# Attention scores with the mask on the moving keys, in a one-core windowed attention and top-1 expert kernel

## What is computed

```python
q = (x @ wq.T + bq).reshape(B, S, H, D)      # k, v likewise
loc = einsum('bnihd,bnjhd->bnihj', qw, kw) * scale          # 32 windows of 128
gsc = einsum('bihd,bjhd->bihj', q[:, gi], k[:, gi]) * scale # gi: 64 global tokens
attn = softmax(scores)          # zeros outside windows and globals
out = einsum('bihj,bjhd->bihd', attn, v) @ wo.T + bo
x = layernorm(x + out)
# experts: argmax of x @ Wg.T picks one of 8; layernorm, scale, bias,
# 256 -> 64, gelu, 64 -> 256; added to x, layernorm again
```

## Time and profile before

| what | value |
|---|---|
| median of 3 executions | 445.81 us (444.01 to 446.04) |
| span of the profiled execution, first to last instruction | 442.8 us |
| the profiled execution's own time | not listed beside its span |
| mean granted clock of TensorE | 0.989 |
| attention steps 2 to 31 | about 46 to 299 us |
| experts | about 299 to 443 us |

### The profile page before, as it was taken

How to read it: one execution, slowest core, us unless ns; L and a number is a source line. 1 busy time by engine, 2 the same in 40 slices (tenths; PEclk the granted TensorE clock), 3 DMA queues, 4 the chain that set the end, 5 groups by cost and what they waited for, 6 DMA issues and landing times.

```text
span 442.8 us, 14658 instructions
## 1 busy us (share of the span) xinstructions
PE 405.3 (92%) x5747; PEld 339.8 (77%) x5747; DVE 326.1 (74%) x796; ACT 250.6 (57%) x523; POOL 220.4 (50%) x301
## 2 busy tenths in 40 slices
PE   5899799999999999999999899988798998999991
PEld 4758678888888888888888778756577887777891
DVE  6785687758757757757759888563668998899785
ACT  3424665675575575575576576676663555544421
POOL 4361343464464464464464566435733485477540
PEclk9999999999999999999999999999989999999997
DMA  8663740000000000000020000000000011011004
GB/s 240 186 199 111 240 137 4 27 25 0 24 24 0 24 24 0 24 24 0 24 72 4 25 2 3 3 1 2 0 2 2 1 49 47 0 47 49 34 15 143
DMA packets 21720, 20.34 MB, mean 46 GB/s; under 512 B 3133, under 2 KB 21682, under 8 KB 21682
## 3 DMA queue, kind: packets, MB, share of 16 engines
q1 hardware_dynamic: 16900, 15.07, 10.9%
q10 hardware_dynamic: 4782, 4.75, 3.3%
HBM read 15.41 MB, written 4.41 MB: 45 GB/s over the span
## 4 chain that ended last, share of the span: by engine, by line
PE 52%; DVE 26%; ACT 9%; issue 8%; DMA 3%; ACTq 1%; DVEq 0%; POOL 0%; POOLq 0%
DVE row_max_t L1154 10%; PE ps L1461 7%; PE ps L1737 7%; PE ps L1424 7%; PE ps L1562 5%; PE ps L1384 5%; PE ps L1415 4%; PE ps L1438 3%; PE ps L1444 3%; ACT probs L847 3%; DVE k_part L1013 2%; ACT boundsT_t L858 2%; PE ps L1406 2%; DMA rows<-in_L_attn_x_dram 2%; ACT k_part L713 2%
## 5 line engine op out<-in xcount | busy, mean ns | idle before, releaser
L847 ACT ACTIVATE probs<-ps 128x1024 f32<-128x1024 f32 x64 | 62.1, 1022 | 68.2 <-PE ps L1428 68.2
L1154 DVE TENSOR_REDUCE row_max_t<-ps 128x16 f32<-128x2048 f32 x31 | 70.9, 2287 | 3.7 <-PE ps L1415 3.6
L1737 PE MATMUL ps<-w_part,hm_part 128*128 128x256 f32 x384 | 53.8, 289 | 1.8 <-DVE hm_part L1332 1.8
L1415 PE MATMUL ps<-k_part,q_part 32*128 32x128 f32 x1584 | 51.5, 274 | 3.1 <-issue 1.5
L1415 PEld LDWEIGHTS ps<-k_part,q_part 32*128 32x128 f32 x1584 | 46.9, 186 | 9.2 <-issue 7.0
L1562 PE MATMUL ps<-xh_parts,w_part 128*128 128x512 f32 x192 | 53.8, 416 | 0.0
L557 POOL TENSOR_TENSOR q_part<-qf,q_part 128x512 fp32r<-128x512 f32 x32 | 41.0, 1281 | 25.7 <-ACT q_part L695 25.7
L599 POOL TENSOR_TENSOR attn_t<-num_t,rden_t 128x256 f32<-128x256 f32 x32 | 20.0, 624 | 64.7 <-DVE rden_t L1185 64.7
L1737 PEld LDWEIGHTS ps<-w_part,hm_part 128*128 128x128 f32 x384 | 48.2, 190 | 4.8 <-DVE hm_part L1332 2.4
L788 ACT ACTIVATE ffn_rows<-ps,b1s 128x512 f32<-128x512 f32 x32 | 22.0, 687 | 42.2 <-PE ps L1562 34.1
L1562 PEld LDWEIGHTS ps<-xh_parts,w_part 128*128 128x128 f32 x192 | 34.7, 194 | 6.5 <-issue 0.6
(11 more groups left out here) (234 smaller groups left out, 906.4 us busy)
## 6 DMA issues: line engine op xcount, KB each, us to landing
table<-rest_sums SPq DMA_DIRECT2D x4, 1088.0 KB, 6.1
xs<-in_L_attn_x_dram SPq DMA_DIRECT2D x16, 256.0 KB, 2.8
rows<-in_L_attn_x_dram ACTq DMA_DIRECT2D x4, 1024.0 KB, 8.1
out_dram<-yout SPq DMA_DIRECT2D x6, 512.0 KB, 2.9
w<-in_L_ffn_W_dram SPq DMA_DIRECT2D x2, 256.0 KB, 7.6
w<-in_L_ffn_W_dram SPq DMA_DIRECT2D x1, 512.0 KB, 4.2
out_dram<-yout SPq DMA_DIRECT2D x2, 256.0 KB, 2.6
out_dram<-yout ACTq DMA_DIRECT2D x2, 256.0 KB, 2.8
```

What stands on the lines that cost most here:

```text
L847: act.activation(probs[:, 2 * h:2 * h + 2, :], ps[:, 2 * h:2 * h + 2, :], ACT.Exp).then_inc(probs_ready, 1)
L1154: dve.tensor_reduce(row_max[:], ps_all, op=ALU.max, axis=AX.X).then_inc(max_ready, 1)
L1415: last = mm(ps[:, u, (2 * c + a) * P:(2 * c + a + 1) * P], q_part[x][quad(u), s, c, a, :], k_part[y][quad(u), s, c, :], start=(i == 0), st ...
L1737: mm(y, hm_part[a][:, 1 - p, f, c * P:(c + 1) * P], w2_part[b][:, f, :], start=(f == 0 and i == 0), stop=False)
```

## The change

Scores: queries are kept whole (`q_whole`, not masked) as the stationary side, and the keys move in two masked copies (`k_masked`, 256 columns): 24 products. The global tokens keep the old form (`scores_of_globals`, 48). Turned scores are as before.

Masks move from DVE to POOL: eight multiplications by a column of `q_scale` per pair of windows (512 elements a partition each), two for each of the high and low part, for keys and queries. `q_low` and the copy of `qf` go. ACT writes the high part of the whole queries from PSUM (two instructions, in the even step, ahead of the exponentials); DVE writes the low part (two instructions, behind the guards).

Order in odd steps: the keys' low part on DVE comes behind the guards; on PE the output product comes ahead of turned scores, and values behind them, next to the second values. On POOL in odd steps the wait for the step's scores and the keys' high part comes first, and the argument of the exponent comes behind a wait for the keys' low part.

`k_masked` lies in a part of `xh_parts`, so the first casts of the expert input move from step 30 to step 31. `w1` lies in `ysum`, so its two loads move from the start to step 24, ahead of `w2`, and its scaling and splitting one step later.

```diff
+        k_masked = [xh_parts[:, 0, i].rearrange("p c n -> p (c n)").rearrange("p (w c a n) -> p w c a n", w=2, c=KC, a=2)
+                    for i in range(2)]
...
-        qf = sb("qf", [P, 2, KC, 2, P])
+        q_whole = [sb(f"q_whole{i}", [P, SLOTS, KC, P], fp32r) for i in range(2)]
...
@@ SP, step 24 (and no longer at the start)
                     sp.wait_ge(rest_ready, NW // 2 + 1)
+                    for c in range(KC):
+                        sp.dma_start(w1[:, c, :, :], w1_dram[:, c * P:(c + 1) * P, :].rearrange("e p h -> p e h")).then_inc(ld_w1, 16)
...
@@ POOL
-            def q_low(w, s):
-                need(pool, turned_scores_in_psum, w - 3)
-                pool.wait_ge(q_high_ready, w // 2 + 1)
-                pool.tensor_tensor(q_part[1][:, s], qf[:, s % 2], q_part[0][:, s].bitcast(fp32), ALU.subtract).then_inc(q_ready, 1)
+            def await_keys_high(w):
+
+                need(pool, scores_in_psum, w)
+                pool.wait_ge(k_high_ready, w // 2 + 1)
...
+            def mask_keys(i, s):
+                for a in range(2):
+                    pool.tensor_scalar(k_masked[i][:, :, :, a, :], k_part[i][:, s:s + 2].bitcast(fp32), q_scale[:, a, 0:1], None,
+                                       ALU.mult).then_inc(k_masked_ready, 1)
+
+            def mask_queries(i, s):
+                for a in range(2):
+                    pool.tensor_scalar(q_part[i][:, s:s + 2, :, a, :], q_whole[i][:, s:s + 2].bitcast(fp32), q_scale[:, a, 0:1], None,
+                                       ALU.mult).then_inc(q_masked_ready, 1)
...
+                keys_due = live(t + 1, steady) and p
+                queries_due = cur and p == 0 and (steady or t > 0)
+                if keys_due:
+                    await_keys_high(t + 1)
+                if queries_due:
+                    await_queries(t)
                 if pp:
...
-                if live(t + 1, steady) and (steady or t > 0):
-                    q_low(t + 1, (s + 1) % SLOTS)
+                if keys_due:
+                    mask_keys(0, (s + 1) % SLOTS)
+                if queries_due:
+                    mask_queries(0, s)
                 if cur:
...
+                    if keys_due:
+                        await_keys_low(t + 1)
                     need(pool, e_ready, t - 1)
...
+                if keys_due:
+                    mask_keys(1, (s + 1) % SLOTS)
+                if queries_due:
+                    mask_queries(1, s)
...
-            q_low(0, 0)
-            q_low(1, 1)
+            pool.wait_ge(dve_const, 4)
+            await_keys_high(0)
+            mask_keys(0, 0)
+            await_keys_low(0)
+            mask_keys(1, 0)
+            await_queries(0)
+            for i in range(2):
+                mask_queries(i, 0)
...
@@ ACT
-                need(act, turned_scores_in_psum, w - 2)
-                act.wait_ge(qf_ready, w // 2 + 1)
-                copy(q_part[0][:, s:s + 2], qf[:]).then_inc(q_high_ready, 1)
+                need(act, turned_scores_in_psum, w - 3)
+                act.wait_ge(q_in_psum, w // 2 + 1)
+                for c in range(KC):
+                    last = act.activation(q_whole[0][:, s:s + 2, c, :], ps_xq[:, c * 2 * P:(c + 1) * 2 * P].rearrange("p (w n) -> p w n", w=2),
+                                          ACT.Identity, bias=bq_col[:, c:c + 1])
...
-                if live(t + 1, steady) and p:
-                    queries_of(t + 1, (s + 1) % SLOTS)
...
+                if ahead and p == 0:
+                    queries_of(t + AHEAD, (s + AHEAD) % SLOTS)
                 if prev:
                     need(act, pv_in_psum, t - 1)
...
@@ DVE
+            def queries_of(w, s):
+
+                dve.wait_ge(q_high_ready, w // 2 + 1)
+                for c in range(KC):
+                    last = dve.scalar_tensor_tensor(q_whole[1][:, s:s + 2, c, :], ps_xq[:, c * 2 * P:(c + 1) * 2 * P].rearrange("p (w n) -> p w n", w=2),
+                                                    bq_col[:, c:c + 1], q_whole[0][:, s:s + 2, c, :].bitcast(fp32), ALU.add, ALU.subtract)
...
-                if live(t + 1, steady) and p:
-                    keys_of(t + 1, (s + 1) % SLOTS)
...
-                    queries_of(t + AHEAD)
+                    queries_of(t + AHEAD, (s + AHEAD) % SLOTS)
+                if live(t + 1, steady) and p:
+                    keys_of(t + 1, (s + 1) % SLOTS)
...
-                if not steady and t == NW - 2:
+                if not steady and t == NW - 1:
                     for pair in range(2):
                         take_high(0, 0, pair)
-                if not steady and t == NW - 1:
                     for k in range(ROUTE_STEPS):
                         route(k, 0)
...
+                    dve.wait_ge(ld_w1, 16 * KC)
...
@@ PE
             def scores(s):
 
                 for c in range(KC):
+                    for i, (x, y) in enumerate(SPLIT):
+                        for u in range(UNITS):
+                            last = mm(ps[:, u, 2 * c * P:(2 * c + 2) * P], q_whole[x][quad(u), s, c, :],
+                                      k_masked[y][quad(u), s % 2, c, :, :].rearrange("p a n -> p (a n)"),
+                                      start=(i == 0), stop=(i == 2), tile_position=(32 * u, 0))
+                return last
...
-                    pe.wait_ge(q_ready, t + 1)
-                    pe.wait_ge(k_ready, t // 2 + 1)
+                    pe.wait_ge(q_ready, t // 2 + 1)
+                    pe.wait_ge(k_masked_ready, 4 * (t // 2 + 1))
...
-                if live(t + 1, steady) and p:
-                    values_of(t + 1)
                 if live(t + 3, steady) and p:
                     turn_x(t + 3)
+                if old and p:
+                    output_product(t - 3)
...
+                    pe.wait_ge(q_masked_ready, 4 * ((t - 1) // 2 + 1))
                     turned_scores((s + 3) % SLOTS).then_inc(turned_scores_in_psum, 1)
...
-                if old:
+                if old and not p:
                     output_product(t - 3)
...
                 if live(t + 1, steady) and p:
+                    values_of(t + 1)
                     second_values()
```

More of the change, by code:

```diff
@@ L180, in windowed_attention_then_top1_experts @@
         rest = sb("rest_t", [P, 2, NV])
+        qgf = rest[:].rearrange("p b n -> p (b n)")[:, 0:2 * HID].rearrange("p (c a n) -> p c a n", c=KC, a=2)
         num = sb("num_t", [P, 2, NV])
@@ L503, in _ @@
             load_w(WO, wo_dram)
-            for c in range(KC):
-                sp.dma_start(w1[:, c, :, :], w1_dram[:, c * P:(c + 1) * P, :].rearrange("e p h -> p e h")).then_inc(ld_w1, 16)
             sp.dma_start(out_bias[:], bo_dram.rearrange("(a n) -> a n", a=1).broadcast_to([P, HID])).then_inc(ld_bo, 16)
@@ L724, in queries_of @@
             def queries_of(w, s):
[L726 to L728 removed]
+                need(act, turned_scores_in_psum, w - 3)
[3 more added lines that the diff above has]
+                                          ACT.Identity, bias=bq_col[:, c:c + 1])
+                last.then_inc(q_high_ready, 1)
             act.wait_ge(xgT_in_psum, 1)
@@ L751, in _ @@
             act.wait_ge(qgf_ready, 1)
-            copy(q_part[0][:, GSLOT], qf[:, 0]).then_inc(qg_high_ready, 1)
+            copy(q_part[0][:, GSLOT], qgf).then_inc(qg_high_ready, 1)
             wide_weight(WV)
@@ L996, in low_of_x @@
                                   x_part[0][:].rearrange("p c w n -> p (c w n)").bitcast(fp32), ALU.subtract).then_inc(x_low_ready, 1)
-            def queries_of(w):
-                need(dve, q_ready, w)
-                dve.wait_ge(q_in_psum, w // 2 + 1)
-                for k in range(2):
-                    for c in range(KC):
-                        last = dve.scalar_tensor_tensor(qf[:, k, c, :, :],
-                                                        ps_xq[:, (2 * c + k) * P:(2 * c + k + 1) * P].unsqueeze(1).broadcast_to([P, 2, P]),
-                                                        bq_col[:, c:c + 1], q_scale[:], ALU.add, ALU.mult)
-                last.then_inc(qf_ready, 1)
+            def queries_of(w, s):
[3 more added lines that the diff above has]
+                                                    bq_col[:, c:c + 1], q_whole[0][:, s:s + 2, c, :].bitcast(fp32), ALU.add, ALU.subtract)
+                last.then_inc(q_ready, 1)
             def keys_of(w, s):
@@ L1018, in _ @@
             for c in range(KC):
-                last = dve.scalar_tensor_tensor(qf[:, 0, c, :, :], ps[:, 6, c * P:(c + 1) * P].unsqueeze(1).broadcast_to([P, 2, P]),
+                last = dve.scalar_tensor_tensor(qgf[:, c, :, :], ps[:, 6, c * P:(c + 1) * P].unsqueeze(1).broadcast_to([P, 2, P]),
                                                 bq_col[:, c:c + 1], q_scale[:], ALU.add, ALU.mult)
@@ L1033, in _ @@
                 count[0] += 1
[L1034 to L1035 removed]
+            queries_of(0, 0)
             keys_of(0, 0)
@@ L1209, in step @@
                     gate_columns()
```

(14 more changed lines are left out.)

21 lines of the change are left out of this document (13 added, 8 removed).

## The result

The changed kernel takes 492.86 us (median of 4, 491.5 to 495.21), the kernel before, on the same chip, 444.91 (443.33 to 446.04): a ratio of 1.109 [1.104 to 1.114], so 11% slower, where 428 and 4% faster was forecast.

The account below looks back on a forecast made before the run. PE, busy 92%, was taken as the bound, nearly tied with DVE's chain; savings of 2.1, 11.5, 3.4 and 2.0 less 1.2 made 17.8 us: 442.8 - 17.8 + 3.0 = 428.0 us, range 422.5 to 438.

Parts of the forecast that it names:

- The price of a mask: POOL's multiplication of 512 elements by a column: taken as 0.66 us, range 0.52 to 1.28, eight per pair of steps.
- rival A: Masks cost 1.28 us like the subtraction, POOL bounds at 16 us of work plus waits a pair: about 451 us; chance 0.07.
- The break point: POOL's masks in the loop: up to 1.0 us each is free; POOL bounds from about 1.2 us.
- Scores: On PE, 48 products of 128 columns become 24 of 256: 1.49 us falls to 0.86, saving 0.63 a step.
- Rival C: Scores on PE cost by columns, so only the reorder is left: about 444 us, no change; chance 0.04.
- The loop, steps 24 to 27, the rest of the attention: Savings: loop 5 x 2.3 = 11.5 us, steps 24 to 27 3.4, steps 1 to 3 2.1, the three to 31 2.0.
- odd-to-even step: Turned scores to turned scores: 8.02 becomes 7.86 us, gain 0.16 only, held by DVE's low part of x.
- even-to-odd step: Turned scores to turned scores: 8.40 becomes 7.65 us, gain 0.75, PE and the maximum's chain in a tie.
- The start: DVE's scaling of the global scores slips by about 0.9 us; POOL's six extra instructions fit into its wait for the bound.
- The end: Early casts no longer hold step 31's maximum (1.0 us) but precede the routing by 1.2: +0.3 us.
- Moved loads, w2, ACT's queries in the loop: w1 loads ahead of w2 at step 24 cost nothing; ACT's query instructions (0.84 us) lie under turned scores, costing nothing.

Follow-up runs that it names:

- experiment 7: Changed kernel with a test behind its last store: six DVE instructions alone, then beside POOL's two-tensor products, column multiplications and copies; 16-element operations 0.18 alone, 1.15 us beside products.
- masks_16: Changed kernel with each mask over 64 elements instead of 512, the rest zeros, score scale 2^-14 of its value (computation partly left out): 441.22 us, ratio 0.993.
- short_mended: Changed kernel with masks over 64 elements, the rest left zero, start and end orders mended, zeros written after the globals' scores: 429.78 us, ratio 0.967 to the kernel before.
- experiment 3: Kernel before with only the reordering (keys' low part behind guards, output product under the maximum, values behind), 48 score products kept: 449.53 us, ratio 1.011.
- experiment 6: Changed kernel, full computation, start and end mended, masks shared over ACT, DVE and POOL; three successive versions: 447.38, 443.57, 435.94 us (ratios 1.007, 0.997, 0.982).

## Why the prediction was wrong, point by point

- **The price of a mask is the step that failed**, as the prediction put it: "Below stands a memset of 512 ... 0.52; above the two-input subtraction, 1.28 ... I take 0.66". Measured: 1.57, above the upper end. The bound rested on the idea that one input can't cost more than two. No row of before had the form, and the row it was priced by (the select) was another form, on 8 partitions. With 1.57 in its own sum of rival A, POOL needs 5.7 + 8 x 1.57 = 18.3 us a pair and with its waits 19 to 20. Measured over the attention: 19.1 us a pair (286.88 / 15) against 16.8 before; 15 pairs at 2.3 more are the 34.4 us. The Trainium skill (GPSIMD Engine Reference, Engine selection) calls one-input operations on POOL roughly line-rate; the runs contradict it for this form (1.56 on POOL, 0.49 on DVE in experiment 7). Its section on cycle accounting gives the 769 ns as the best case of a tight loop, not as the price of this instruction; it is half of what was measured.
- **The price was not the only step that failed.** With masks of 0.45 and 0.93 us the change as made took 441.22 and 446.81 us, on either side of the assumed 0.66, where 428 was forecast. The two terms for the start and the end, 1.2 us together, were some 13 us in `masks_16` (7.3 and 5.6) and 15.6 in the changed kernel.
- **Rival A** had the mechanism and a chance of 0.07. Its time of 451 was too low even at its own price: at 1.29 a pair took 17.8 us, 15.7 of work and 2.1 of waits (0.7 for the step's own scores, 0.75 for the keys' low part, the rest for the two guards), where about 1 was allowed.
- **The break point was right only in part.** "m up to 1.0 is free": masks of 0.93 cost 6.8 us more over the attention than masks of 0.45 (244.27 against 237.44). "It decides from m of about 1.2": at 1.29 the attention is 20 us longer than before, but POOL still waits 12% of the loop.
- **Scores**: forecast 0.86 for 24 products of 256 columns, read 0.91 to 0.92 (160.41 to 161.32), so 0.57 to 0.58 saved instead of 0.63. Rival C falls.
- **The loop, steps 24 to 27, the rest of the attention**: with cheap masks 31.46 us per four steps (forecast 31.0), 32.45 for steps 24 to 27 (31.3) and 16.4 us in all in the traces (17.8 forecast). The turned scores of `short_mended` stand 7.82 and 7.84 apart (144.02 to 151.84, 136.18 to 144.02), forecast 7.65 and 7.86: the odd-to-even step came as worked out, the even-to-odd step gained 0.58 instead of 0.75. That 429.78 stands so near 428.0 is in part luck. On its own chip the gain of the medians is 14.1 us (443.83 less 429.78), the masks were cheaper (0.45) than the 0.66 of the sum and did not do their work, and the edges had been mended. The attention gained 15.7 us where the terms add up to 19.0, and start and end lost almost nothing where 1.2 were allowed.
- **The start** was forecast to cost 0.9 and cost 8.6. "POOL's six extra instructions there fit into its wait for the bound" was priced at 0.66 each; eight at 1.57 end at 32.8, and the shift that was at 26.6 comes behind. And ACT's new instructions were costed as time ("0.84") without asking what was queued behind their wait: `x_rest`. Ahead of both, PE waits 2.35 us for the keys' masks before the scores of step 0. Mended with short masks, the loss is 0.2.
- **The end** was forecast to cost 0.3 and cost 7.0. Missed: the output product, moved ahead of turned scores, waits in step 31 for an ACT that has extra work there; the casts ahead of the routing make the selection late; and PE runs there at the lower clock level (in the trace of after the output product at 336.59 takes 2.08 us at a granted 0.50, elsewhere 1.03). Only the first of these has a run of its own (experiment 3, 4.5 us); the others are argued.
- **Moved loads, w2, ACT's queries in the loop** cost nothing visible, as said.

## What to carry to other kernels

Price an instruction form that no row shows by a run, or leave the range open above: fewer inputs is no upper bound. Where an engine gets eight new instructions a pair, ask first how long it may take before it is the bound (here about 1 us each), and how likely its price lies above that. When an instruction is moved in front of others, list what waits behind it in the odd first and last steps too, not only in the loop; here mending them gave back 8 of 48 us. And a mask that an almost idle engine does for free may be paid for by another engine: look for tiny operations that take a microsecond.

## What the hardware showed that was not expected

- POOL's multiplication by a column or a constant: 1.56 and 1.49 us for 512 elements, slower than with two tensors (1.26) and 2.5 times a copy (0.61).
- DVE operations with two inputs in SBUF, and copies, casts and scalings there, are held up by POOL: 16 elements took 1.15 and 1.18 us beside products of two tensors instead of 0.18 and 0.17, the reduction (0.17) and the copy from PSUM (0.42) kept their times; a cast of 8 elements took 1.27 instead of 0.16 (experiment 6). The Trainium skill (SBUF — State Buffer, Who interferes with whom) has the rule that the two engines share a pair of ports, that a reduction, and an operation with at most one input from SBUF outside DVE's two-port modes, does not contend, and that the side that comes second is blocked for a whole instruction. The probe agrees, but for one row: the scaling of 16 elements took its 0.17 beside the column form too.
- One DVE operation of 16 elements was kept out over five POOL products, 7.33 us, and the same one in `short_mended` for 4.59 us, until two long memsets on POOL had ended. The probe's back-to-back products never did this, and why is open.
- Moving a product ahead of two masks on POOL, meant to free PE earlier, cost 16 us.
